# A graph network on one core: the edge matrix holds (weight, gate) pairs, a fourth layer uses it, and TensorE spreads the source numbers

## What is computed

```python
# src, dst sorted by dst; edge_weight, edge_weight1: one number per edge
support = segment_sum(edge_weight[:, None] * x[src], dst)            # layer 0
h = relu(concat([x, support]) @ L0_W + L0_b)
...                                                                  # layer 1: two attention layers
msgs = edge_weight[:, None] * (x @ L2_weight + L2_bias)[src]         # layer 2, "weighted"
out = segment_sum(msgs, dst)
gate = sigmoid(mlp(edge_weight1))                                    # layer 3, three GCN layers
deg = segment_sum(gate, dst) + 1
agg = segment_sum(h[src] * (dinv[src] * gate * dinv[dst])[:, None], dst)
return agg + h * (1.0 / deg)[:, None]
```

## Time and profile before

| | us |
|---|---|
| median of 3 runs (7494.9 to 7497.09) | 7495.76 |
| span of the profiled execution | 7496.3 |
| busy: PE / PEld / DVE / ACT / POOL | 5794.1 / 4263.8 / 3503.5 / 1542.9 / 5305.8 |

### The profile page before, as it was taken

How to read it: one execution, slowest core, us unless ns; L and a number is a source line. 1 busy time by engine, 2 the same in 40 slices (tenths; PEclk the granted TensorE clock), 3 DMA queues, 4 the chain that set the end, 5 groups by cost and what they waited for, 6 DMA issues and landing times. The chain is left out here.

```text
span 7496.3 us, 123067 instructions
## 1 busy us (share of the span) xinstructions
PE 5794.1 (77%) x30182; PEld 4263.8 (57%) x30182; DVE 3503.5 (47%) x13968; ACT 1542.9 (21%) x5084; POOL 5305.8 (71%) x5079
## 2 busy tenths in 40 slices
PE   3777777776628888867777766666699979998998
PEld 2444444445516555556666655555566656675665
DVE  4555555554446666645555533333222222232444
ACT  2333333331202222212222222222100000110001
POOL 3777777777657777657777567777577767776776
PEclk9888888887869999955555578999899999999998
DMA  8888888883224444423333234434477767766775
GB/s 262 185 153 160 156 157 152 153 151 118 89 74 117 116 116 117 108 69 84 83 77 83 72 110 117 118 118 117 154 245 235 238 191 241 241 214 216 242 243 178
DMA packets 693853, 1137.56 MB, mean 152 GB/s; under 512 B 139288, under 2 KB 441804, under 8 KB 691060
## 3 DMA queue, kind: packets, MB, share of 16 engines
q0 software_dynamic: 301456, 555.10, 33.1%
q1 hardware_dynamic: 389860, 552.91, 22.6%
q10 hardware_dynamic: 2304, 26.74, 0.8%
HBM read 889.84 MB, written 244.48 MB: 151 GB/s over the span
## 5 line engine op out<-in xcount | busy, mean ns | idle before, releaser
L900 POOL DMA_INDIRECT rows<-gcn_rows,index x1632 | 1547.9, 948 | 611.0 <-issue 466.2
L1434 POOL DMA_INDIRECT rows<-gat_rows,index x1568 | 1501.6, 958 | 642.8 <-issue 461.6
L1764 POOL DMA_INDIRECT support<-rows,index x784 | 1215.1, 1550 | 383.0 <-DMA support<-rows,index 219.7
L1565 PE MATMUL bank<-onehots,rows 128*128 128x128 f32 (+1 forms) x4704 | 945.8, 338 | 326.8 <-DVE rows L1641 326.6
L986 PEld LDWEIGHTS bank<-onehots,rows 128*128 128x128 f32 x6528 | 853.6, 193 | 421.3 <-issue 359.2
L1565 PEld LDWEIGHTS bank<-onehots,rows 128*128 128x128 f32 (+1 forms) x4704 | 721.2, 202 | 527.0 <-issue 327.3
L986 PE MATMUL bank<-onehots,rows 128*128 128x128 f32 x6528 | 882.1, 278 | 117.0 <-DVE onehots L1038 77.1
L676 POOL DMA_INDIRECT rows<-norm,index x784 | 742.6, 947 | 286.1 <-issue 225.1
L999 PE MATMUL dense_bank<-matrix,edge_space 128*128 128x512 f32 x1536 | 722.7, 593 | 0.0
L1881 PE MATMUL rows_bank<-x_window,cross 128*128 128x256 f32 x1568 | 615.1, 478 | 87.1 <-ACT cross L1865 86.8
L732 PE MATMUL bank<-onehots,rows 128*128 128x128 f32 x3136 | 485.9, 313 | 228.7 <-DVE onehots L763 204.1
(11 more groups left out here) (323 smaller groups left out, 8427.2 us busy)
## 6 DMA issues: line engine op xcount, KB each, us to landing
matrix<-matrix SPq DMA_DIRECT2D x96, 1024.0 KB, 7.0
edge_space<-gcn_rows SPq DMA_DIRECT2D x138, 512.0 KB, 9.5
alpha<-matrix SPq DMA_DIRECT2D x51, 1024.0 KB
dst_row<-in_dst_flat SPq DMA_DIRECT2D x100, 512.0 KB
source_row<-in_src_flat SPq DMA_DIRECT2D x99, 512.0 KB, 6.4
matrix<-zeros SPq DMA_DIRECT2D x196, 256.0 KB
support<-zeros ACTq DMA_DIRECT2D x16, 1632.0 KB, 28.0
rows<-gcn_rows,index POOLq DMA_INDIRECT x1632, 5.7
```

Source lines behind the costliest of these rows:

```text
L900: nc.gpsimd.indirect_dma_start(rows[:, k, :], None, table, bass.IndirectOffsetOnAxis(ap=index[:, k:k + 1], axis=0),).then_inc(gathered[k], 16)
L1434: nc.gpsimd.indirect_dma_start(rows[:, k, :], None, table, bass.IndirectOffsetOnAxis(ap=index[:, k:k + 1], axis=0),).then_inc(gathered[k], 16)
L1565: done = nc.tensor.matmul(to, left, onehots[:, k, :], start=first and c == 0, stop=final and c == chunks - 1)
L1764: nc.gpsimd.indirect_dma_start(support[k % COPIES], bass.IndirectOffsetOnAxis(ap=index[:, k // HALF, k % HALF:k % HALF + 1], axis=0), rows ...
```

## The change

1. The dense matrix has (weight, gate) pairs: 8 bytes for each entry, 1,024 numbers for each partition and step. `write_matrix` writes pairs, and the zeros are twice as long.
2. Layer 2 runs as a `dense_pass` with `WeightedBlock`; `edge_pass` is gone. The matmul of a step reads every second number of the loaded matrix (`value` 0 or 1).
3. In `dense_pass` the steps lie in 7 slots, each loaded by itself, and each step releases its slot. `sync_start` stands ahead of the first loads. SP's stores and loads are placed by tile.
4. The own rows are added by DVE, no longer by PE: `ScaledBlock` loses 2 matmuls of 128x128 (those with `acc`) for each block, `LastBlock` one of 128x256, `WeightedBlock` one of 128x256.
5. In `scatter_by_source` `source_row` comes from PE: a matmul of a broadcast column with the identity for each tile, 4 to a bank, and an ACT copy of 128x512. The broadcast DMA goes.
6. The sums over equal edges are made by PE (`add_same`, 15 matmuls with 2 moving columns for each turn) from comparisons by DVE (`compare`, 7 for each turn). `tail_step` and `gate_row` go.

```diff
@@ ScaledBlock
-    def pe_first(self, pe, s, j, b, runs):
-            matmul(to, self.own_rows[:, c * P:(c + 1) * P], identity, start=c == 0, stop=False)
-            done = matmul(to, identity, self.g.acc[:, c, nodes_of(b)], start=False, stop=c == 1)
+            done = self.nc.tensor.matmul(by_chunk(self.turned)[:, c, :], self.own_rows[:, c * P:(c + 1) * P],
+                                         self.g.identity[:], start=c == 0, stop=c == 1)
+    def dve_first(self, dve, s, j, b, runs):
+        dve.wait_ge(s.turned, j + 2)
+        dve.wait_ge(s.added, runs)
+        here = by_chunk(self.turned)
+        self.nc.vector.tensor_tensor(here, here, self.g.acc[:, :, nodes_of(b)], ALU.add).then_inc(s.own_added, 1)
@@ dense_pass
+    def stages_of(blocks_in_turn):
+        if ends.stages == 3:
+            return ((3, 9, 13),) if blocks_in_turn == 1 else ((2, 7, 9), (10, 14, 15))
+        return ((3, 9),) if blocks_in_turn == 1 else ((2, 6), (8, 13))
...
+                def load_step(q):
+                    n, row = q % SLOTS, q % steps_of_group
...
+                        sync.wait_ge(s.steps_used, before + 1 - before // steps_of_group)
+                    sync.dma_start(matrix[n], by_step[:, q, :]).then_inc(step_loaded[n], 16)
+                    sync.dma_start(table_rows[:, n, :], table[nodes_of(row), :]).then_inc(step_loaded[n], 16)
+
+                ends.sync_start(sync, s)
                 sync.wait_ge(g.matrix_written, 16 * (g.real_tiles - g.turns * RING))
...
+                                                matrix[n].rearrange("p (n v) -> p n v", v=2)[:, :, value],
@@ scatter_by_source
-                        sync.wait_ge(s.matrices, i * RING + HALF * (h + 1))
-                        sync.dma_start(
-                            source_row[:, h, :, :].rearrange("p k e -> p (k e)"),
-                            g.source_flat[0:1, bass.ds((i * 2 + h) * (HALF * P), HALF * P)]
-                            .to_broadcast([P, HALF * P])).then_inc(row_loaded[h], 16)
+                def source_rows(half, batch):
...
+                    for n in range(BATCH):
+                        column = source_columns[:, batch * BATCH + n:batch * BATCH + n + 1].to_broadcast([P, P])
+                        done = nc.tensor.matmul(row_bank[:, n * P:(n + 1) * P], column, g.identity[:], start=True,
+                                                stop=True)
+                    done.then_inc(s.row_turned, 1)
+                def copy_row(half, h, batch):
+                    act.wait_ge(s.row_turned, half * 2 + (batch + 1))
...
+                    nc.scalar.copy(source_row[:, h, batch * BATCH:(batch + 1) * BATCH, :].rearrange("p k e -> p (k e)"),
+                                   row_bank[:]).then_inc(s.row_ready, 1)
-                    dve.wait_ge(row_loaded[h], i * 16 + 16 * (ahead + 1))
+                    dve.wait_ge(s.row_ready, i * 4 + (2 * (2 * ahead + h) + 2))
@@ build_program
-        edge_pass(nc, g, norm2, edge_weight, WeightedBlock, factor=t.L2_gnn_weight, bias=t.L2_gnn_bias,
+        dense_pass(nc, g, norm2, 0, WeightedBlock, factor=t.L2_gnn_weight, bias=t.L2_gnn_bias,
```

More of the change, by code:

```diff
@@ L490, in pe_start, with pe_first, pe_second @@
         pe.wait_ge(s.loaded, 64)
[L492 to L496, removed]
+    def pe_first(self, pe, s, j, b):
+        pe.wait_ge(s.used, j + 1)
+        pe.wait_ge(s.sums_ready, j + 1)
         for c in range(2):
-            matmul(to, self.sums[:, c, :], self.factor[:, c, :], start=c == 0, stop=False)
-        matmul(to, self.g.identity[:], x_of(self.g, b), start=False, stop=True).then_inc(s.multiplied, 1)
-    def pe_second(self, pe, s, b):
-        pe.wait_ge(s.normal_ready, b + 1)
-        pe.wait_ge(s.left_ready, b + 1)
+            done = self.nc.tensor.matmul(self.product[:, 0:self.g.features], self.sums[:, c, :], self.factor[:, c, :],
+                                         start=c == 0, stop=c == 1)
+        done.then_inc(s.multiplied, 1)
+    def pe_second(self, pe, s, j, b):
+        pe.wait_ge(s.normal_ready, j + 1)
+        pe.wait_ge(s.left_ready, j + 1)
         for c in range(2):
@@ L602, in pe_start, with pe_first @@
         pe.sem_inc(s.multiplied, 1)
-    def pe_first(self, pe, s, j, b, runs):
-        matmul, identity, to = self.nc.tensor.matmul, self.g.identity[:], self.product[:, 0:self.g.features]
-        pe.wait_ge(s.own_loaded, j * 16 + 16)
+    def pe_first(self, pe, s, j, b):
         pe.wait_ge(s.used, j + 1)
         pe.wait_ge(s.sums_ready, j + 1)
-        matmul(to, identity, self.own_rows[:], start=True, stop=False)
         for c in range(2):
-            done = matmul(self.product[:, c * P:(c + 1) * P], self.sums[:, c, :], identity, start=False, stop=c == 1)
+            done = self.nc.tensor.matmul(self.product[:, c * P:(c + 1) * P], self.sums[:, c, :], self.g.identity[:],
+                                         start=c == 0, stop=c == 1)
         done.then_inc(s.multiplied, 1)
-    def pe_second(self, pe, s, j, b):
-        pass
     def act_start(self, act, s):
@@ new lines, in keep_totals, with copy_columns @@
+                def keep_totals(i):
+                    act.wait_ge(s.same_used, i * NEAR + (NEAR + 2))
+                    act.sem_inc(s.issued, 1)
+                    nc.scalar.copy(g.matrix_value[:, bass.ds(i * TAIL_BATCH, TAIL_BATCH), :], totals
+                                   ).then_inc(s.near_ready, 1)
+                def copy_columns(half):
+                    if not isinstance(half, int):
+                        act.wait_ge(s.row_turned, half * 2)
+                    act.sem_inc(s.issued, 1)
+                    nc.scalar.copy(source_columns[:], g.source_float[:, bass.ds(half * HALF, HALF)]
+                                   ).then_inc(s.columns_ready, 1)
@@ L3370, in build_program @@
     planes = dram("planes", [heads, slots])
-    g.matrix = dram("matrix", [GROUPS * g.rows * P * GROUP, 1])
+    g.matrix = dram("matrix", [GROUPS * g.rows * P * GROUP, 2])
     with ExitStack() as stack:
```

547 lines of the change are left out of this document (202 added, 345 removed).

## The result

| | us |
|---|---|
| forecast | 7230 (7130 to 7360), slower: 0.07 |
| changed kernel, median of 4 | 7573.6 (7559.7 to 7577.7) |
| before, median of 4 beside it | 7496.4 |
| ratio | 1.0098 (95% interval 1.0084 to 1.0113) |
| span of the profiled execution, granted clock | 7575.9, 0.842 |

A forecast was written before the change was run, and what follows sets the result against it. It took POOL as the bound, at 1.25 us a gather tile in the layers, with PE nearly as full and above POOL in the new layer 2. 7496.3 - 239 (layer 2) - 26 (GCN layers) = 7231, say 7230 us; range 7130 to 7360.

The forecast's parts named there:

- I take **0: Scatter loop: no net change; bounds a gain of 110 us or a loss of 75 us, at 1.5 us a turn.
- at 1.2 GHz the 25.7 would be 51: Scatter loop: PE's work of 25.7 us a turn, against POOL's 29.6, would be 51 at the low clock.
- The likeliest error: Scatter loop, where three engines' order changed and it was priced at nothing; then the stalls of layer 2.
- The same bytes in the same bursts, so the waits for scatters stay: Scatter loop: 4 x 512 KB of zeros a turn replace source numbers and smaller zeros; waits for scatters unchanged.
- 239 forecast: Layer 2 as a dense pass: 720 us plus ends of 58 make 778, against 1017.4; bounds 262 and 137 less.
- the 720 to the last gather: Layer 2 without ends: 727 us with PE's stalls, some 700 with them covered; 720 taken.
- The stops in turns with two blocks: Layer 2: PE stops 2.3 us in each of 13 turns with two blocks, 30 us in all.
- My third rival: Layer 2: the ends stop PE in every turn, some 100 us more, 7330 us; chance 0.12.
- 26 less forecast: GCN layers: 13 us less for each of the two `ScaledBlock` layers, bounds 0 and 15 each; `LastBlock` 0.
- rival 2: All four dense layers: gathers land too late, 7366 us at 12.25 us landings; sign, POOL's waits for ACT's index; chance 0.13.
- Rival 1: Dense layers' steps: PE reads the pairs at half rate, 3.4 us a step for 1.71, 8460 us; chance 0.05.
- stays at 1.71: Dense layers: by the skill's cacheline rule the strided read keeps full rate, a step stays at 1.71 us.

The follow-up runs named there:

- three-edit one: Changed kernel with source rows two tiles earlier, two own-row buffers and two buffers for the last layer's normalised rows: 7216.1 us, ratio 0.9619.
- experiment 9: Against the base, a step's matmul reads the first 512 loaded numbers without stride, same bytes, output not the reference's: 7222.7 us, ratio 0.9632.
- experiments 11 and 13: First: the base with two own-row buffers, 7224.0 us. Second: that plus four `same_edge` buffers and two `normal` buffers in `LastBlock`, 7233.2 us.
- experiment 15: Against the three-edit one, the `tail_row` load moved behind the first half turn's loads in SP's queue: 7195.8 us, ratio 0.9594.
- experiment 12: Against the base, gather indices copied two turns ahead instead of one: 7259.8 us, ratio 0.9677; layer 2 812.3 us.
- experiment 10: Against experiment 9, SP loads only the first 512 of a step's 1,024 numbers (2 KB runs, 256 KB): 7195.7 us, ratio 0.9590.
- the base: Changed kernel with PE's source-row matmuls two tiles earlier and ACT's row copies at tiles 1 and 3: 7261.7 us, ratio 0.9682.

## Why the prediction was wrong

**The scatter loop is the step that failed.** I wrote that DVE's "wait for the DMA becomes a wait for PE and ACT that comes every half turn" and "I take **0**", with a loss of at most 75 us. It cost 258, 5.3 us a turn. My sum of PE's work was not the fault: with the rows in time the same work fits into 31.1 us a turn (1523 / 49). What I left out is the loop of dependence that the new wait closes. PE's rows feed DVE's scans, which stand in DVE's queue ahead of the one-hots that PE needs next. DVE's lead of four tiles does not help, since the copy is released at PE's fifth tile. Nobody's busy time shows this; a sum of one half turn along the chain would have. PE's five tiles, the 8 rows' matmuls and the sums that stand ahead of them (3 matmuls in one half turn, 8 in the other, 5.5 in the mean) at full clock are 5 x 1.16 + 8 x 0.24 + 5.5 x 0.20 = 8.8 us (rows and sums from PE's timeline: 0.98 us for 4, 0.59 for 3), and 6.0 to 6.3 from the rows to the restart make 14.8 to 15.1. POOL's half turn is 14.8. So at full clock the chain is level with the bound engine or just over it, and at half clock it is 23.6 to 23.9. The measured half turn, 18.7 in the mean, lies between: with 3 sums it took 15.6 us (1005.65 to 1021.29), which leaves 21.8 for one with 8. And PE pauses in every half turn, and comes back at the low clock. I had the low clock in the text ("at 1.2 GHz the 25.7 would be 51") and bounded the loss by 1.5 us a turn, which came from no row. Two tiles earlier take 2 x 1.16 us and the sums' share off the chain, and it stays under POOL's time.

The likeliest error was named rightly; its chance of 0.07 for slower, and above all its bound, were not.

**The zeros.** "The same bytes in the same bursts, so the waits for scatters stay" can't be read off one run, because the source DMA went as the zeros doubled. Apart, 1 MB more a turn costs 83 us in the kernel before and 109 in the three-edit one. With the rows in time, the exchange and the rest of parts 5 and 6 together gave 54 us (1576.6 to 1523.0), which I had inside a bound only (110).

**Layer 2: 239 forecast, 204 measured.** The mechanism was right (PE bounds it, ends 59.1 us against 58), the 720 to the last gather was 754.7. The strided step gives 196 x 0.09 = 17.6 of the 35. The stops in turns with two blocks were sized rightly: up to the last gather (4570 to 5325 us) PE's waits for DVE's one-hots and ACT's sums are

```profile
PE bank L832 <- DVE onehots L881: 19.9, 13, 2.8
PE product L502 <- ACT sums L357: 7.0, 7, 1.2
```

With one of 1.0 for `normal` that is 28 us, where I had 30. But I let part of them be covered when I went from 727 us down to 720: 7 of the 35. The other 10 were not separated; PE is busy for 712 us up to there, and 697 - 9 + 17.6 = 706 is what I should have had. My third rival, stops in every turn, did not come.

**The GCN layers: 26 less forecast, 38 more measured.** What I counted on came: PE's first wait fell from 28.1 us to 15.9 and POOL's stop of 6.6 us went. Against it stood three things that I had at nothing: the strided read, 17.6 us of PE a layer, of which 5 to 10 showed in the time (experiment 9); the own rows and the stores, which SP now issues among loads of twice the size into single buffers, and which came late (18 and 14 us, and 22 in the last layer, by experiments 11 and 13). With those buffers the three layers take 2121.7 us (experiment 15), 32 under before, though the read is still strided: from first to last gather the first of them takes 680.5 us, which is POOL's 544 x 1.25 = 680, so PE is no longer its bound. The gain of 26 was there to be had.

**Twice the matrix.** Gathers landed after 5.1 us, less than before (6.0), not 6 to 9; rival 2 did not come. Its sign, POOL's waits for ACT's index, did: 75.5 us in layer 2, and in the GCN layers 16.4, 16.8 and 28.2 where they were 9.1, 9.8 and 4.9. In layer 2 they are covered by PE (experiment 12), in the first GCN layer they fall to 5.7 with two buffers for the own rows, with all the bytes. The bursts are smaller (640 KB for 1.5 MB), which may be why gathers land sooner; it wasn't tested. By the rule of the Trainium skill (DMA: Bandwidth & Descriptors, Queues, rings and completion order) of whole packets in turn a gather should be held up longer beside longer runs. The 5.1 against 6.0 goes the other way, but the bursts changed too; where the pieces come in the same order and only their runs and bytes are halved (experiment 10), gathers in layer 2 land after 3.8 us in place of 4.8, as the rule has it. Bytes and runs were not told apart. What the bytes did delay are the small loads in SP's own queue.

**Half rate for the strided read.** Rival 1 did not come, and neither did "stays at 1.71": a record of 512 columns takes 0.45 us, not 0.43. The Trainium skill (SBUF — State Buffer, the note on cachelines) has full rate for two reads of each 16-byte line; measured is 5% less, 1.80 against 1.72 us a step in two kernels that differ in the read alone (the base, 5200.15 to 5201.95, and experiment 9).

## What to carry to other kernels

When a wait for a DMA becomes a wait for an engine, close the loop: write down one period from the new producer through every queued instruction to the producer's own next input, and compare that with the bound engine's period, at TensorE's low clock too if there is a pause in it. Put what feeds another engine's queue first in the period, not where there is room. Look in SP's queue for what stands behind a wait that moved, and give small loads and stores a second buffer when the loads around them grow.

## What the runs showed of the hardware

- Pauses of TensorE of about 2 us could bring back its low clock. After 1.85 us a 128x256 matmul in two records took 1.22 us in place of 0.70, at once; after one of 2.17 us the first operations were still fast and those from 1.2 us on slow. From 600 to 1400 us all 43 stops of the changed kernel (1.85 to 2.17 us) were followed by the low clock within 4 us, and of the base kernel's 52 (1.2 to 2.2 us, 1.4 in the mean) 10 were; the mean clock is 0.77 and 0.93. The length of the pause does not decide alone: of the 20 stops of 1.8 to 2.6 us that the kernel before made from full clock in that window, 9 were not followed by the low one.
- A 128x512 fp32 matmul whose moving operand takes every second number runs 5% slower than one that reads on: records 0.45 us apart in place of 0.43.
- DMAs of zeros to DRAM are not free beside scatters: 1 MB more for each turn of 31 to 32 us, on some 160 GB/s moved, lengthened the turn by 1.7 us in one kernel and 2.2 in another.
